# Gated cross-attention with a mixture of experts on one core: expert tiles of 128 rows in place of 256, and one PSUM bank each for gate and up

## The reference, cut to what matters

```python
x = x + tanh(g_xattn) * xattn(layernorm(x), ctx, ...)      # 16 x 112 rows of 256
x = x + tanh(g_ffn) * ffn(layernorm(x), ...)

def ffn(x):                       # D_MODEL, D_FF, N_EXPERTS, TOP_K = 256, 512, 8, 2
    probs = softmax(xf @ router_w.T)                       # n = 1792 rows, 8 experts
    topv, topi = top_k(probs, 2)                           # the others' weight is 0
    g = einsum('nd,edf->nef', xf, gate_w) + gate_b
    u = einsum('nd,edf->nef', xf, up_w) + up_b
    h = silu(g) * u
    expert_out = einsum('nef,efd->ned', h, down_w) + down_b
    y = einsum('ne,ned->nd', probs, expert_out)
```

## Time and profile before

| | |
|---|---|
| three runs | 672.1, 678.1 and 675.3 us, median 675.3 |
| span of the profiled execution | 669.9 us |
| attention and routing | up to about 451 us |
| expert stage, first tile's load done to the last gathered row | about 454 to 648 us |
| last stage | about 648 to 670 us |
| TensorE, VectorE, ScalarE, GpSimd busy | 489.1, 441.8, 317.2, 272.3 us |

### The profile page before, as it was taken

One profiled execution on the slowest core, in us unless ns is written; L12 is line 12 of the kernel. 1 busy time (PEld: TensorE's weight loads), 2 busy tenths in 40 slices (PEclk: granted clock), 3 DMA queues, 4 the chain that ended last, 5 costly groups with the idle time before them and its releaser, 6 DMA issues. The chain is left out here.

```text
span 669.9 us, 14994 instructions
## 1 busy us (share of the span) xinstructions
PE 489.1 (73%) x4678; PEld 441.9 (66%) x4679; DVE 441.8 (66%) x920; ACT 317.2 (47%) x566; POOL 272.3 (41%) x244
## 2 busy tenths in 40 slices
PE   3378578998899999899988300008999999999910
PEld 2367477887888888788867200006999999999810
DVE  1755378786888988899988598603555555555417
ACT  1332355664657767667656542504444444444301
POOL 9302255552454455554545158860222222222223
PEclk9688699897999999999989655557999999999965
DMA  8438566677788868877420547823121222221038
GB/s 182 130 95 232 129 154 158 161 230 204 180 233 230 219 187 207 240 187 190 124 49 3 201 159 243 290 81 126 54 62 61 63 63 63 63 63 48 33 99 261
DMA packets 82169, 96.43 MB, mean 144 GB/s; under 512 B 27240, under 2 KB 67648, under 8 KB 82000
## 3 DMA queue, kind: packets, MB, share of 16 engines
q1 hardware_dynamic: 78576, 86.71, 47.5%
q0 software_dynamic: 3552, 9.19, 3.9%
HBM read 62.80 MB, written 32.96 MB: 143 GB/s over the span
## 5 line engine op out<-in xcount | busy, mean ns | idle before, releaser
L346 POOL TENSOR_TENSOR PL<-PT 125x448 f16<-125x448 f32 x96 | 100.2, 1046 | 145.8 <-ACT PT L468 145.7
L732 DVE TENSOR_REDUCE mx<-bank 112x1 f32<-112x375 f32 x256 | 130.7, 542 | 43.2 <-PE bank L566 41.0
L468 ACT ACTIVATE PT<-bank 125x448 f32<-125x448 f32 x192 | 103.8, 544 | 91.7 <-PE bank L581 91.2
L1277 POOL DMA_INDIRECT y_scr<-ys,where x42 | 40.3, 959 | 153.1 <-DVE ys L1387 146.7
L566 PE MATMUL bank<-KS,QS 97*112 97x376 f32 x256 | 90.0, 374 | 13.9 <-DVE mx L732 11.4
L581 PE MATMUL bank<-QS,KS 98*125 98x256 f32 x384 | 84.0, 304 | 14.6 <-DMA QS<-nm 13.3
L1375 DVE SCALAR_TENSOR_TENSOR hf<-bank,ub,sg 128x256 f32<-128x256 f32 x84 | 39.2, 483 | 62.9 <-ACT sg L1299 62.9
L581 PEld LDWEIGHTS bank<-QS,KS 98*125 98x125 f32 x384 | 66.7, 193 | 16.6 <-DMA QS<-nm 9.7
L1299 ACT ACTIVATE sg<-bank,gb,inv 128x256 f32<-128x256 f32 x84 | 42.8, 560 | 73.4 <-PE bank L1334 73.4
L1334 PE MATMUL bank<-xH,GH 128*128 128x256 f16 x336 | 64.9, 275 | 0.8 <-DVE xL L1367 0.5
L1334 PE MATMUL bank<-xL,GH 128*128 128x256 f16 x336 | 64.9, 275 | 0.0
(11 more groups left out here) (203 smaller groups left out, 1110.2 us busy)
## 6 DMA issues: line engine op xcount, KB each, us to landing
KS<-k_scr SPq DMA_DIRECT2D x48, 376.0 KB
k_scr<-kH SPq DMA_DIRECT2D x16, 376.0 KB, 2.8
k_scr<-kL SPq DMA_DIRECT2D x16, 376.0 KB, 3.7
xs_scr<-empty SPq DMA_DIRECT2D x9, 642.5 KB, 9.1
xt<-xs_scr SPq DMA_DIRECT2D x21, 257.0 KB
QS<-q_scr SPq DMA_DIRECT2D x96, 56.0 KB, 5.0
ctx_sb<-in_ctx SPq DMA_DIRECT2D x16, 281.2 KB
wsq<-in_L_ffn_gate_w SPq DMA_DIRECT2D x8, 512.0 KB, 4.6
```

What stands on the lines that cost most here:

```text
L346: pool.tensor_tensor(PL[:, 2 * k:2 * k + 2, :, 0:N], PT[:, 2 * k:2 * k + 2, :, 0:N], PH[:, 2 * k:2 * k + 2, :, 0:N], ALU.subtract).then_in ...
L468: act.activation(PT[:, 2 * k:2 * k + 2, :, 0:N].rearrange("p a e i -> p (a e) i"), psST[k % 2][0:JP].rearrange("p (a i) -> p a i", i=NI)[: ...
L732: dve.tensor_reduce(mx[:, hd:hd + 1], psS[hd % 2][0:N, 0:M], AX.X, ALU.max).then_inc(v_max, 1)
L1277: pool.indirect_dma_start(y_scr, bass.IndirectOffsetOnAxis(ap=where[:, t % UN, k:k + 1].bitcast(mybir.dt.uint32), axis=0), ys[:, u, k, :], ...
```

## The change

`TS` is 128 in place of 256. That makes 35 tiles of 128 rows, 4480 rows in all, in place of 21 of 256, 5376 rows. The scratch behind `xs_scr` is filled in blocks of 4 x 128 rows in place of 5 x 128. Since four parts of 128 columns fill a bank, gate and up of a tile have one bank each, and the two banks of either alternate by tile. TensorE does all of gate, then all of up, and tells of each with a semaphore of its own (`k_G`, `k_U`); ScalarE waits for gate, VectorE for up.

```diff
-    TS = 256
+    TS = 128
     NT = TOP_K * B * N // TS + E - 1
-    EK = 5
+    EK = 4
...
-        k_T, k_GU, k_D = sem("pe_tileT"), sem("pe_gate_up"), sem("pe_down")
+        k_T, k_G, k_U, k_D = sem("pe_tileT"), sem("pe_gate"), sem("pe_up"), sem("pe_down")
...
-        FB = 512 // TS
-        FQ = FC // FB
...
-                        wait(act, k_GU, FQ * (t - 1))
+                        wait(act, k_U, t - 1)
...
+                        act.wait_ge(k_G, t + 1)
                         for f in range(FC):
-                            act.wait_ge(k_GU, FQ * t + f // FB + 1)
                             wait(act, v_h, FC * (t - 1) + f + 1)
-                            act.activation(sg[:, f, :], bG[f // FB][:, TS * (f % FB):TS * (f % FB + 1)], ACT.Silu,
+                            act.activation(sg[:, f, :], bG[u][:, TS * f:TS * (f + 1)], ACT.Silu,
...
-                        for q in range(FQ):
-                            wait(pe, a_s, FC * (t - 1) + FB * (q + 1))
-                            wait(pe, v_h, FC * (t - 1) + FB * (q + 1))
-                            for j, bank in enumerate((bG[q], bU[q])):
-                                for f in range(FB * q, FB * (q + 1)):
-                                    for n, (W, x) in enumerate(((GH, xH), (GH, xL), (GL, xH))):
-                                        for k in range(DC):
-                                            w = W[:, bass.ds(e1, 1), j, k, 128 * f:128 * (f + 1)]
...
-                            mm.then_inc(k_GU, 1)
+                        for j, (bank, spent, left, full) in enumerate(((bG, a_s, FC, k_G), (bU, v_h, FC, k_U))):
+                            wait(pe, spent, left * (t - 1))
+                            for f in range(FC):
+                                for n, (W, x) in enumerate(((GH, xH), (GH, xL), (GL, xH))):
+                                    for k in range(DC):
+                                        w = W[:, bass.ds(e1, 1), j, k, 128 * f:128 * (f + 1)]
+                                        mm = pe.matmul(bank[u][:, TS * f:TS * (f + 1)],
+                                                       w.rearrange("p o f -> p (o f)"), x[:, u, k, :],
+                                                       start=(n == 0 and k == 0), stop=(n == 2 and k == DC - 1))
+                            mm.then_inc(full, 1)
...
+                        dve.wait_ge(k_U, t + 1)
                         for f in range(FC):
                             dve.wait_ge(a_s, FC * t + f + 1)
-                            dve.scalar_tensor_tensor(out=hf[:, f, :], in0=bU[f // FB][:, TS * (f % FB):TS * (f % FB + 1)],
+                            dve.scalar_tensor_tensor(out=hf[:, f, :], in0=bU[u][:, TS * f:TS * (f + 1)],
```

More of the change, by code:

```diff
@@ L1325, in step @@
                         pe.wait_ge(v_x, t + 1)
-                        for q in range(FQ):
-                            wait(pe, a_s, FC * (t - 1) + FB * (q + 1))
-                            wait(pe, v_h, FC * (t - 1) + FB * (q + 1))
-                            for j, bank in enumerate((bG[q], bU[q])):
-                                for f in range(FB * q, FB * (q + 1)):
-                                    for n, (W, x) in enumerate(((GH, xH), (GH, xL), (GL, xH))):
-                                        for k in range(DC):
-                                            w = W[:, bass.ds(e1, 1), j, k, 128 * f:128 * (f + 1)]
-                                            mm = pe.matmul(bank[:, TS * (f % FB):TS * (f % FB + 1)],
-                                                           w.rearrange("p o f -> p (o f)"), x[:, u, k, :],
-                                                           start=(n == 0 and k == 0), stop=(n == 2 and k == DC - 1))
-                            mm.then_inc(k_GU, 1)
+                        for j, (bank, spent, left, full) in enumerate(((bG, a_s, FC, k_G), (bU, v_h, FC, k_U))):
[8 more added lines that the diff above has]
+                            mm.then_inc(full, 1)
                     if has(i, c, 2):
```

## The result

The changed kernel took 710.26 us (median of 4 runs, 705.43 to 713.42), the kernel before 676.69 us beside it (4 runs, 672.08 to 680.36): slower, by 33.6 us on the medians, which is 5.0%. Over the undisturbed executions alone it is 1.056 times as long, with a 95% interval of 1.050 to 1.061. Forecast were 709 us and a range of 699 to 726.

What follows compares the result with a forecast made beforehand. TensorE's array bound the kernel before, sequencer issue after: +35.6 us from first gate to last down, -1.9 for start and tail, +34. Profiled span 669.9 + 34 = 704; the median, 5.4 higher, 709. Range 699 to 726.

Steps and rivals of the forecast that it cites:

- The bound: Expert stage after the change: TensorE bound by issue, 6.2 us of sequencer against 4.3 of array a tile; chance 0.78.
- A register instruction with its matmuls: TensorE's sequencer in gate, up and down: 0.12 us for a register instruction together with the matmuls issued beside it.
- A tile, 6.0 us and 7.1 at the loop's head: TensorE's sequencer time for one 128-row tile: 6.0 us, with 1.1 extra each of the loop's seven runs.
- +35.6 predicted: From the first gate matmul to the last of down: 182.3 us before, 218 after.
- Before the stage: Scratch filling and three routing operations ahead of the expert stage: taken as 0, at most 0.5 us either way.
- The ends: Start and tail of the expert stage together -1.9 us; the last down's wait for `hL` about as late as before.
- +34: Whole change in time: +35.6 from first gate matmul to last of down, -1.9 for start and tail.
- The wait for all of up: VectorE's first product waits for all of up; chain at most 4.6 us against TensorE's 6.0, so hidden.
- The array's pace: Rival: register instructions issued at the array's pace, 4.3 us a tile, some 648 us in all; chance 0.06.
- The clock: Rival: pauses lower TensorE's clock, some 775 us, or 720 to 760 for parts of the stage; chance 0.06.
- The longer chain: Rival: ScalarE and VectorE chain exceeds 6.0 us, a tile about 6.5, 718 to 728 us; chance 0.07.
- The free time of the sequencer before: Kernel before: sequencer needs 6.4 us a tile, 6.7 with loop extra, under the array's 8.5, so wholly hidden.

Runs made afterwards that it cites:

- experiment 1: Changed kernel with expert 0's gate and up weights at a fixed address for every tile, without their 32 register instructions: 651.76 us, ratio 0.968 to the kernel before.
- experiment 3: Changed kernel with expert 0's down weights at a fixed address for every tile, without down's eight register instructions: 680.88 us, ratio 1.012 to the kernel before.
- experiment 5: Changed kernel with one more, unused reading of the tile's expert in TensorE's sequencer each step: 735.47 us, ratio 1.092 to the kernel before.
- experiment 7: Kernel before the change with five more unused readings of the expert in each step: 735.62 us, ratio 1.093 to the kernel before.
- experiment 2: Kernel before the change with expert 0's gate and up weights at a fixed address for every tile: 674.84 us beside 674.26, ratio 0.999.
- experiment 6: Kernel before the change with two more unused readings of the expert in each step: 684.53 us, ratio 1.017 to the kernel before.
- experiment 8: Changed kernel with comparisons branching to one of eight fixed-address copies of the gate and up matmuls, replacing 32 register instructions: 904.28 us, ratio 1.344 to the kernel before.

## Why the prediction was right

**The bound.** It named issue by TensorE's sequencer, from a place where the sequencer ran free and one where it was ahead. Experiments 1, 3 and 5 show this bound directly: taking away 32 or 8 register instructions a tile saves 61 and 29.5 us, adding one reading costs 22.

**A register instruction with its matmuls, 0.12 us.** Measured 0.123 in gate and up. Matmul by matmul, the shorter groups of six come at distances of 0.118, 0.124, 0.064, 0.056, 0.056 and 0.056 us, 0.474 together, where 0.48 was predicted; every second group takes 0.03 to 0.05 more, between its first two matmuls, and why stays open.

**A tile, 6.0 us and 7.1 at the loop's head.** Measured 5.97 to 6.17, 6.07 on the mean, some early ones 6.2 to 6.3, and 7.3 at the loop's head. The term that was too small is this one: I had rounded the tile down from 6.1, because the distances "lie nearer 0.118", and they are 0.123 on the mean. In its parts, gate and up take 3.9 us where I had 3.84, down 0.96 as I had it, and the 0.15 for the five matmuls that need no address instruction is not there: the head starts 0.11 us after down's last one, the ordinary distance. About 0.07 us for each of 35 tiles (2.5 together), a loop's head that costs 1.25 where I had 1.1 (1.1 over the seven) and a pause of 0.8 behind the loop's end, which I had not counted, make most of the difference between the +35.6 predicted and the +40.9 measured.

**Before the stage.** I took 0 for it; 64.0 us against 64.3 from the last matmul of the attention to the last scatter bear that out.

**The ends.** The last down waits 1.15 us for `hL`, about as before, as predicted. The start gave 0.9 us where I had 0.4, the tail 1.8 where I had 1.5. So the stage came to +38.2 against +34. The measured medians differ by 33.6, less than the stage in the traces, but the part before the stage scatters by more than that difference, and the ratio of 1.056 is +38 on 674 us. That the predicted time lies 1.3 us from the measured median is thus partly luck; what the traces confirm is +34 to within some 4 us.

**The wait for all of up.** `hf` waits 86 us on TensorE in the stretch, and no pause of TensorE in that stretch ends by it, as the prediction's chain of 4.6 us under 6.0 had it. VectorE's time for a tile fell to 2.7 us (93.0 over 34 tiles), below the 4 named. Taken alone, the alternating banks are a gain of 17 to 20 us, which I had not priced: the prediction compared only the tile of 256 rows in two halves with the new scheme.

**The rivals.** The array's pace: experiment 1 reaches it, 4.37 us a tile, and only without the addresses. The clock: 0.99 in the stage. Experiment 7 shows that it was no empty threat: with pauses of 1.8 us or more ahead of each tile it fell in some of them. The longer chain: no pause of TensorE but the last ends by VectorE.

**The free time of the sequencer before.** "Wholly hidden" was right for the kernel as it stood (experiment 2), but the means of 6.4 against 8.5 us overstate the room: experiment 6 had 1.3 us a tile added, under the 2.1 us that seemed free, and its stage lost 7.5 us.

## What to carry to other kernels

When a tile is made smaller, list what is issued once for a step or once for a weight, whatever the rows: here 40 register instructions and a head. Their price for each row doubles, and they go from hidden to bounding. Find the sequencer's own pace where the array is not in its way, at the start of a stage or after a wait, and hold its time for a tile against the array's before halving anything. And count as cover for a step's head only the lead that the queue gives (2 us here), not the whole free time of the tile.

## What the runs showed of the hardware

- A busy share near 100% for TensorE (208 of 219 us) stood for an array that was fed every 0.08 us and could take every 0.056 (experiment 1). The listed length of a matmul overlaps its neighbours; the pace is read from the distances of starts (0.08 and 0.056 us beside a listed length of 0.22 to 0.23).
- A reading of a number into a register costs TensorE's sequencer 0.63 us (22.1 / 35, experiment 5), five times an address instruction (0.123).
- Comparisons that branch to one of eight far copies took up to 4.5 us, with 2.18 MB of instructions moved in place of 0.38 (experiment 8). A fetch of the target's code is the reading that fits; it was not isolated.
- With a pause of 1.8 us or more ahead of every tile, TensorE's granted clock fell in some tiles (0.86 and 12.2 us in experiment 7) and not in others (1.00 and 10.6 us).

Open: whether the address instructions can be made fewer for tiles of 128 rows, for one by letting the rows be the stationary operand and the weights stream in wider pieces. It was not tried. With the weights held still as here, the 652 us of experiment 1 are what is left when all address instructions of gate and up are gone.
